# Tiles of exponentials that hold one tile of keys of two heads, and a nan made by multiplication

## The chip, the cores and the metric

The kernel runs on one core of a Trainium2 chip. The metric is the device time of one execution in microseconds; less is better. The engines are called as in the profile: PE (TensorE, matmuls), DVE (VectorE), ACT (ScalarE), POOL (GpSimd), SP (SyncE, which only issues DMAs).

## What is computed

Four batches of 512 tokens of width 256 go through four blocks of cross attention to 1024 context tokens and a feed-forward each. Cut to what matters here (names shortened):

```
x = x + tanh(g_xattn[0]) * attention0(layernorm(x), ctx)   # 16 heads of 16, 512 queries, 1024 keys
x = x + tanh(g_ffn[0])   * ffn0(layernorm(x))              # binarized weights, gelu
x = x + tanh(g_xattn[1]) * attention1(layernorm(x), ctx, mask)
x = x + tanh(g_ffn[1])   * ffn1(layernorm(x))              # x and weights to float8_e4m3fn, then a product
x = x + tanh(g_xattn[2]) * attention2(layernorm(x), ctx)   # one head
x = x + tanh(g_ffn[2])   * ffn2(layernorm(x))
x = x + tanh(g_xattn[3]) * attention3(layernorm(x), ctx)   # as attention0
x = x + tanh(g_ffn[3])   * ffn3(layernorm(x))              # six layers of local attention and a gated ffn

# attention0, 1, 3, for each batch and head:
scores = einsum('bhqd,bhkd->bhqk', q, k) / sqrt(16)        # layer 1: where(mask, scores, -inf)
ctx = einsum('bhqk,bhkd->bhqd', softmax(scores), v)

# ffn1, its quantization (beyond 464 the cast gives nan):
x_q = (x.astype(float32) / s_in).astype(float8_e4m3fn)
k_q = (kernel.astype(float32) / s_k).astype(float8_e4m3fn)
```

## The kernel before

The program has two parts. first_part computes everything up to the last block's cross attention, last_part the six layers of ffn3. Only first_part matters here.

**Units and groups.** The heads of layers 0, 1 and 3 are worked off in 12 units, one for each layer and batch, in that order; a unit has 4 groups of 4 heads. first_order writes the order of all work by hand: every step gets a turn (put), a unit has 64 turns, a group 16, and each engine's program walks through the same list and takes from it what is its own. Each turn of a group has one step M and one step E, where E runs LAG = 20 turns behind M.

- **M** (scores with queries on the partitions): two matmuls at L428 write 128 queries x 1024 keys of one head to a pair of PSUM banks; DVE takes the row maximum (L651, in layer 1 L648 with the mask added).
- **sh** (L438, L669, L671, two DMAs): the 16 x 128 maxima of a group are transposed, negated and written by DMA as two more rows of the stacked queries. E of that group needs them.
- **E** (scores with keys on the partitions, shifted by the maxima): two matmuls at L449, in layer 1 with the mask added by one more each (L452), fill a pair of PSUM banks, and ACT writes their exponentials, 128 x 1024, to one of six tiles of probs (L831). Before the change such a tile is **two tiles of 128 keys of one head**, 512 queries each.
- **PV** (L465): the product with the values, 32 columns of the array for each head, so that four heads lie side by side. A burst is eight matmuls (2 tiles of keys x 4 heads), each of which PE does in two passes, so it shows as x16. It needs four E tiles and comes after the sixth. A group has 4 bursts, all 12 units 192. The result lies in one bank (acc) until **T** (L838, ACT) copies it; then DVE shuffles and inverts the sums in four pieces (L678, **R** L684).

Three pairs of PSUM banks go round between M, E and two similar steps (plan for "two"), two single banks between PV and all the rest (plan for "one"). M and E alternate, so an E takes the pair of the M of two turns before, when DVE has its maximum, and an M the pair of the E of the turn before, when ACT has its exponentials.

**Fillers.** Between them stand the projections of the next unit (L410, then ACT L817, L821, L825), values (L418, DVE L623), the output projection (L474), layer norms (L382, L389, L398), and beside units 2 to 5 ffn0 (L489, L496), beside units 6 to 9 ffn1, attention2 and ffn2 (L504 to L561).

**quantize** (L566 on) turns 128 x 512 values into float8_e4m3fn on DVE, step by step, each after the one before: where a value is beyond 464 the result must be nan, and that is made by L581 (1 or 0), L583 (the reciprocal: 1 or infinity), L586 (the difference with itself: 0 or nan), L588 (added to the result). It runs nine times: once on ffn1's weights (step qw), and for each batch on two chunks of 512 (step q1), whose product is L504. A row maximum of M stands between the two of a batch in DVE's queue, and others behind them.

## Time and profile before

| | us |
|---|---|
| median of 3 runs | 5603.79 |
| lowest and highest | 5603.43, 5604.02 |
| profiled execution | 5599.21 |
| its span, first to last instruction | 5597.9 |
| PE busy in the span | 4956.6 (89%) |
| DVE busy | 3445.9 (62%) |
| ACT busy | 3134.1 (56%) |
| POOL busy | 2262.1 (40%) |

The span is that of the profiled execution alone, and the other times have no profile. The start of an instruction is in microseconds from the span's start. Idle time of an engine is counted from the end of its last instruction to the start of the next, and a matmul's end lies some way behind the start of the next one in a stream, so a stall of PE is longer than the idle time beside it. The granted clock is a share of 2.4 GHz: 0.50 is 1.2 GHz.

### The profile page before, as it was taken

What the parts mean: (1) busy time and instruction counts of PE and PEld (TensorE: products, weight loads), DVE (VectorE), ACT (ScalarE), POOL (GpSimd) and SP (SyncE); (2) the same over time, 40 slices, a digit from 0 to 9 for tenths busy, and PEclk for the clock granted to TensorE, in tenths of its full rate; (3) what the DMA queues carried; (4) which work ended last, traced back from release to release, by engine and by line L of the source; (5) the groups of instructions that cost most, each with busy time, mean ns of one, the idle gap of its engine ahead of it and who ended that gap; (6) DMA issues with size and microseconds to landing.
All of it is one profiled execution on the core that took longest, in us unless ns stands there. A gap on an engine that the chain in (4) does not pass through costs nothing.

```text
span 5597.9 us, 92896 instructions
## 1 busy us (share of the span) xinstructions
PE 4956.6 (89%) x35848; PEld 3090.5 (55%) x35848; DVE 3445.9 (62%) x6534; ACT 3134.1 (56%) x6626; POOL 2262.1 (40%) x2202
## 2 busy tenths in 40 slices
PE   5888889979797878886999999999999999999997
PEld 2233323334343433323877777777777777777775
DVE  4664556574756565674766666666666666666664
ACT  2554454434343434444767677666767776676762
POOL 1111011001010101103867676667767666676762
PEclk6999999989898988997999999999999999999998
DMA  4232223221221111321100000000000000000000
GB/s 100 45 58 46 41 51 63 39 60 41 55 45 40 35 40 38 56 33 36 34 13 18 21 20 20 18 19 25 19 21 20 20 18 19 24 20 17 20 13 31
DMA packets 125064, 189.00 MB, mean 34 GB/s; under 512 B 18800, under 2 KB 67568, under 8 KB 124400
## 3 DMA queue, kind: packets, MB, share of 16 engines
q1 hardware_dynamic: 124624, 183.06, 14.7%
q8 instruction: 285, 4.67, 0.4%
q14 instruction: 155, 1.27, 0.1%
HBM read 150.09 MB, written 32.51 MB: 33 GB/s over the span
## 4 chain that ended last, share of the span: by engine, by line
PE 65%; DVE 18%; ACT 9%; issue 5%; POOL 2%; DMA 1%; SPq 0%; DVEq 0%; ACTq 0%; POOLq 0%
PE psum L1210 15%; PE psum L1258 8%; PE psum L465 6%; PE psum L1259 4%; PE psum L428 4%; PE psum L449 3%; DVE maxes L651 3%; ACT probs L831 2%; PE psum L1267 2%; PE psum L1300 2%; PE psum L1291 2%; PE psum L410 2%; PE psum L1282 2%; PE psum L474 2%; DVE psum L1415 1%
## 5 line engine op out<-in xcount | busy, mean ns | idle before, releaser
L831 ACT ACTIVATE probs<-psum 128x1024 f32<-128x1024 f32 x768 | 767.3, 1020 | 674.2 <-PE psum L449 388.4
L651 DVE TENSOR_REDUCE maxes<-psum 128x1 f32<-128x1024 f32 x512 | 615.0, 1212 | 336.1 <-PE psum L428 332.2
L1401 DVE TENSOR_TENSOR lwork<-psum,rotary 128x512 f32<-128x512 f32 x384 | 265.2, 691 | 779.9 <-ACT lwork L1503 743.4
L1528 ACT ACTIVATE lprobs<-psum,small_stats,stats 128x128 f32<-128x128 f32 x1536 | 579.8, 460 | 196.9 <-DVE small_stats L1419 196.0
L1588 POOL TENSOR_TENSOR stats<-stats,minus_half 128x8 f32<-128x8 f32 x384 | 640.4, 1668 | 32.0
L1584 POOL TENSOR_TENSOR lwork<-lwork 128x512 f32<-128x512 f32 x384 | 493.1, 1284 | 328.6 <-DVE lwork L1403 328.6
L428 PE MATMUL psum<-stack 96*128 96x512 bf16 x1536 | 485.7, 399 | 152.8 <-ACT probs L831 121.5
L449 PE MATMUL psum<-stack 98*128 98x512 bf16 x1536 | 520.6, 395 | 107.8 <-DVE maxes L651 58.2
L930 POOL TENSOR_TENSOR attn<-attn,sums 128x512 f32<-128x512 f32 x48 | 60.8, 1266 | 1316.6 <-DVE sums L684 1316.6
L1503 ACT ACTIVATE lwork<-psum 128x512 f32<-128x512 f32 x384 | 231.2, 602 | 382.7 <-PE psum L1259 382.2
L648 DVE CUSTOM_DVE_ANT_0 psum<-psum,mask_by_query 128x1024 f32<-128x1024 f32 x256 | 314.0, 1229 | 195.8 <-PE psum L428 194.8
L1258 PE MATMUL psum<-wqkv_hi,xs_hi 128*128 128x512 f32 x768 | 339.8, 442 | 87.0 <-DVE att_lo L1433 43.5
L465 PE MATMUL psum<-probs,values 128*32 128x512 f32 x3072 | 397.4, 638 | 2.5 <-ACT probs L831 2.5
L428 PEld LDWEIGHTS psum<-stack 96*128 96x128 bf16 x1536 | 131.1, 100 | 433.5 <-ACT probs L831 227.2
L449 PEld LDWEIGHTS psum<-stack 98*128 98x128 bf16 x1536 | 141.1, 101 | 411.0 <-DVE maxes L651 126.9
L1258 PE MATMUL psum<-wqkv_hi,xs_lo 128*128 128x512 f32 x768 | 307.7, 401 | 0.0
L1258 PE MATMUL psum<-wqkv_lo,xs_hi 128*128 128x512 f32 x768 | 305.4, 398 | 0.0
L1300 PE MATMUL psum<-mixed_vals,turned 128*64 128x65 f32 x3072 | 261.0, 227 | 33.7 <-DVE lwork L1403 33.0
L1415 DVE TENSOR_REDUCE psum<-psum 128x4 f32<-128x512 f32 x384 | 265.3, 691 | 1.3 <-PE psum L1282 1.3
L1300 PEld LDWEIGHTS psum<-mixed_vals,turned 128*64 128x64 f32 x3072 | 207.8, 137 | 102.4 <-issue 53.4
L915 POOL TENSOR_TENSOR ln_stats<-ln_stats,minus_half 128x4 f32<-128x4 f32 x32 | 32.2, 1007 | 572.7 <-DVE ln_stats L609 572.7
L1409 DVE TENSOR_REDUCE stats<-lwork 128x8 f32<-128x512 f32 x384 | 263.3, 686 | 0.3 <-issue 0.3
(228 smaller groups left out, 12530.1 us busy)
## 6 DMA issues: line engine op xcount, KB each, us to landing
stack<-k_parts SPq DMA_DIRECT2D x288, 128.0 KB
staged<-in_quads SPq DMA_DIRECT2D x144, 256.0 KB, 2.4
k_parts<-parts SPq DMA_DIRECT2D x48, 384.0 KB, 2.8
stack<-q_parts SPq DMA_DIRECT2D x288, 64.0 KB
staged<-in_w SPq DMA_DIRECT2D x54, 256.0 KB, 2.7
ctx<-in_ctxT SPq DMA_DIRECT2D x24, 512.0 KB, 4.8
q_parts<-parts SPq DMA_DIRECT2D x24, 384.0 KB, 2.8
arena<-in_ctxT SPq DMA_DIRECT2D x8, 512.0 KB, 4.3
```

The costliest lines, as they stand in the source:

```text
L428: ins = tensor.matmul(ps[:, i, :], q[0:STACK, h, qt * P:(qt + 1) * P], k[0:STACK, h, i * S:(i + 1) * S], start=True, stop=True)
L449: ins = tensor.matmul(ps[:, i, :], ky[0:STACK + 2, h, kt * P:(kt + 1) * P], q[0:STACK + 2, h, :], start=True, stop=L != 1)
L465: ins = tensor.matmul(bank(acc)[32 * h:32 * h + 32, :], values[:, kt, 4 * g + h, :], pr, start=kt == 0, stop=kt == KT - 1)
L651: ins = vector.tensor_reduce(to, pair(("M", u)), AX.XY, ALU.max)
L831: scalar.activation(probs[:, i % 6, :, :], pair(("E", u)), ACT.Exp).then_inc(S_["E_act"], 1)
L1210: ins = tensor.matmul(ps, l, r, start=first and n == 0, stop=last and n == 2)
L1258: tensor.matmul(qk, x_[:, c, b % 2, tok(tt)], w_[:, c * COLS:c * COLS + 512], start=first, stop=last)
L1300: ins = tensor.matmul(bank(("pv", u, 0))[64 * w:64 * w + 64, h * (LHD + 1):(h + 1) * (LHD + 1)], pt[:, h, 64 * w:64 * w + 64], (va if w el ...
L1415: step(vector.tensor_reduce(top, scores(u), AX.X, ALU.max))
L1528: ins = scalar.activation(pr[:, h, :], scores(u)[:, h % 2, h // 2, :], ACT.Exp, bias=st[:, 4 + h:5 + h], scale=y[:, h:h + 1])
L1584: gpsimd.tensor_tensor(t1, t1, t2, ALU.add)
L1588: pool_step(gpsimd.tensor_tensor(st[:, 8:16], st[:, 0:8], minus_half[:, :], ALU.pow))
```

## The change

There are two edits, independent of each other.

**The tiles.** An E tile is now one tile of 128 keys of two heads (kt, and p for heads 2p and 2p + 1) in place of two tiles of keys of one head. So two E tiles, not four, complete a tile of keys for all four heads, and PV runs for each of the eight tiles of keys, four matmuls at a time, from two tiles of probs. Its turn is two behind the second E tile, as before: turn 2 kt + 3 of the group's E in place of 4 k + 5. ACT's wait for a free tile of probs, the values' and masks' waits and the loads' waits follow. T is written one turn earlier. The accumulator's bank is taken at the group's turn 3 in place of 5.

**The nan.** L581 gets a second operation, minus 1, so it gives 0 or -1; L583, the reciprocal, becomes a tensor_scalar that multiplies twice by 3e38, which gives 0 or minus infinity.

```diff
@@ -141,17 +141,17 @@
         put(16 * n - 12 if n > 2 else -1, ("st", u))
     for n, (L, b) in enumerate(UNITS):
         for i in range(64):
-            g, h, qt = i // 16, i % 16 // 4, i % 4
-            put(64 * n + i, ("M", (L, b, g, h, qt)))
-            put(64 * n + i + LAG, ("E", (L, b, g, h, qt)))
+            g, j = i // 16, i % 16
+            put(64 * n + i, ("M", (L, b, g, j // QT, j % QT)))
+            put(64 * n + i + LAG, ("E", (L, b, g, j // 2, j % 2)))
         for g in range(G4):
             t = 64 * n + 16 * g
             if L == 1:
                 put(t + 16, ("sha", (L, b, g)))
             put(t + 17, ("sh", (L, b, g)))
-            for k in range(KT // 2):
-                put(t + LAG + 4 * k + 5, ("PV", (L, b, g, k)))
-            put(t + LAG + 19, ("T", (L, b, g)))
+            for kt in range(KT):
+                put(t + LAG + 2 * kt + 3, ("PV", (L, b, g, kt)))
+            put(t + LAG + 18, ("T", (L, b, g)))
             for i in range(QT):
                 put(t + LAG + 20 + i, ("R", (L, b, g, i)))
         for k in range(KT // 2):
@@ -437,33 +437,31 @@
                     left(one, ("sh", u), PE)
                     tensor.transpose(bank(("sh", u))[0:16, 0:P], maxes[:, n % 4, 0:16], ident[:, :]).then_inc(S_["sh_pe"], 1)
                 elif stage == "E":
-                    L, b, g, k2, h = u
+                    L, b, g, kt, p = u
                     n = group_of[L, b, g]
                     PE.wait_ge(shift_in[n % 4], 32 * (n // 4 + 1))
                     if L == 1:
-                        PE.wait_ge(S_["mc_dve"], at_("mc", (b, 4 + k2)))
+                        PE.wait_ge(S_["mc_dve"], at_("mc", (b, 4 + kt // 2)))
                     left(two, ("E", u), PE)
                     ps, q, ky = pair(("E", u)), qst[n % 3], kst[n % 3]
                     for i in range(2):
-                        kt = 2 * k2 + i
+                        h = 2 * p + i
                         ins = tensor.matmul(ps[:, i, :], ky[0:STACK + 2, h, kt * P:(kt + 1) * P], q[0:STACK + 2, h, :],
                                             start=True, stop=L != 1)
                         if L == 1:
                             ins = tensor.matmul(ps[:, i, :], ident_b[:, :], masks_k[:, kt * S:(kt + 1) * S], start=False, stop=True)
                     ins.then_inc(S_["E_pe"], 1)
                 elif stage == "PV":
-                    L, b, g, k2 = u
-                    PE.wait_ge(S_["va_dve"], at_("va", (L, b, k2)))
-                    PE.wait_ge(S_["E_act"], at_("E", (L, b, g, k2, 3)))
+                    L, b, g, kt = u
+                    PE.wait_ge(S_["va_dve"], at_("va", (L, b, kt // 2)))
+                    PE.wait_ge(S_["E_act"], at_("E", (L, b, g, kt, 1)))
                     acc = ("acc", (L, b, g))
-                    if k2 == 0:
+                    if kt == 0:
                         left(one, acc, PE)
-                    for i in range(2):
-                        for h in range(4):
-                            kt = 2 * k2 + i
-                            pr = probs[:, tile_of((L, b, g, k2, h)) % 6, i, :]
-                            ins = tensor.matmul(bank(acc)[32 * h:32 * h + 32, :], values[:, kt, 4 * g + h, :], pr,
-                                                start=kt == 0, stop=kt == KT - 1)
+                    for h in range(4):
+                        pr = probs[:, tile_of((L, b, g, kt, h // 2)) % 6, h % 2, :]
+                        ins = tensor.matmul(bank(acc)[32 * h:32 * h + 32, :], values[:, kt, 4 * g + h, :], pr,
+                                            start=kt == 0, stop=kt == KT - 1)
                     ins.then_inc(S_["PV_pe"], 1)
                 elif stage == "wo":
                     L, b, m = u
@@ -578,9 +576,9 @@
             step.join()
             step(vector.scalar_tensor_tensor(out=big, in0=val, scalar=16.0, in1=big, op0=ALU.is_ge, op1=ALU.mult))
             step.join()
-            step(vector.tensor_scalar(val, val, 464.0, None, ALU.is_le))
+            step(vector.tensor_scalar(val, val, 464.0, 1.0, ALU.is_le, ALU.subtract))
             step.join()
-            vector.reciprocal(aux, val)
+            vector.tensor_scalar(aux, val, 3e38, 3e38, ALU.mult, ALU.mult)
             step(vector.tensor_tensor(big, big, lo8, ALU.add))
             step.join()
             step(vector.tensor_tensor(aux, aux, aux, ALU.subtract))
@@ -616,7 +614,7 @@
                     L, b, k2 = u
                     n = unit_of[L, b]
                     if n:
-                        V.wait_ge(S_["PV_pe"], at_("PV", UNITS[n - 1] + (3, k2)))
+                        V.wait_ge(S_["PV_pe"], at_("PV", UNITS[n - 1] + (3, 2 * k2 + 1)))
                     V.wait_ge(S_["va_pe"], at_("va", u))
                     for k in range(2):
                         heads = lambda x: x.rearrange("p (h d) -> p h d", h=H)
@@ -630,7 +628,7 @@
                     if b and i < 4:
                         V.wait_ge(S_["M_dve"], at_("M", (1, b - 1, 3, 3, i)))
                     elif b:
-                        V.wait_ge(S_["E_pe"], at_("E", (1, b - 1, 3, i - 4, 3)))
+                        V.wait_ge(S_["E_pe"], at_("E", (1, b - 1, 3, 2 * (i - 4) + 1, 1)))
                     dst = masks_q if i < 4 else masks_k
                     vector.tensor_scalar(dst[:, i % 4 * S2:(i % 4 + 1) * S2], mask_u8[:, j % 2, :], -1.0, -MASKED,
                                          ALU.add, ALU.mult).then_inc(S_["mc_dve"], 1)
@@ -827,12 +825,12 @@
                     i = tile_of(u)
                     A.wait_ge(S_["E_pe"], at_("E", u))
                     if i > 5:
-                        A.wait_ge(S_["PV_pe"], (i - 6) // 4 + 1)
+                        A.wait_ge(S_["PV_pe"], (i - 6) // 2 + 1)
                     scalar.activation(probs[:, i % 6, :, :], pair(("E", u)), ACT.Exp).then_inc(S_["E_act"], 1)
                 elif stage == "T":
                     L, b, g = u
                     n = group_of[u]
-                    A.wait_ge(S_["PV_pe"], at_("PV", (L, b, g, 3)))
+                    A.wait_ge(S_["PV_pe"], at_("PV", (L, b, g, KT - 1)))
                     if n > 3:
                         A.wait_ge(S_["wo_pe"], at_("wo", UNITS[n // 4 - 1] + (1,)))
                     scalar.activation(outs[:, g, :], bank(("acc", (L, b, g))), ACT.Copy).then_inc(S_["T_act"], 1)
@@ -975,7 +973,7 @@
                         i = at_("pj", (L, b, j)) - 1
                         SP.wait_ge(parts_out[i % 3], 16 * (i // 3 + 1))
                     if n > 2:
-                        SP.wait_ge(S_["E_pe"], at_("E", GROUPS[n - 3] + (3, 3)))
+                        SP.wait_ge(S_["E_pe"], at_("E", GROUPS[n - 3] + (KT - 1, 1)))
                     k, q = kst[n % 3], qst[n % 3]
                     rows = slice(g * 4 * HD, (g + 1) * 4 * HD)
                     for i, (pq, pk) in enumerate(PAIRS):
```

How the order on the engines changes, at three places.

PE in the first unit of layer 0, among the projections of the next one (L410), before; L449 is E, L428 is M:

```order
L410 MATMUL psum<-ctx,w_att 128x512 x2
L449 MATMUL psum<-stack 128x512 x2
L428 MATMUL psum<-stack 128x512 x2
L449 MATMUL psum<-stack 128x512 x2
L428 MATMUL psum<-stack 128x512 x2
L410 MATMUL psum<-ctx,w_att 128x512 x2
L449 MATMUL psum<-stack 128x512 x2
L428 MATMUL psum<-stack 128x512 x2
L449 MATMUL psum<-stack 128x512 x2
L428 MATMUL psum<-stack 128x512 x2
L465 MATMUL psum<-probs,values 32x512 x8
L410 MATMUL psum<-ctx,w_att 128x512 x2
```

and now (the bursts are L463):

```order
L410 MATMUL psum<-ctx,w_att 128x512 x2
L449 MATMUL psum<-stack 128x512 x2
L428 MATMUL psum<-stack 128x512 x2
L449 MATMUL psum<-stack 128x512 x2
L428 MATMUL psum<-stack 128x512 x2
L463 MATMUL psum<-probs,values 32x512 x4
L410 MATMUL psum<-ctx,w_att 128x512 x2
L449 MATMUL psum<-stack 128x512 x2
L428 MATMUL psum<-stack 128x512 x2
L449 MATMUL psum<-stack 128x512 x2
L428 MATMUL psum<-stack 128x512 x2
L463 MATMUL psum<-probs,values 32x512 x4
L410 MATMUL psum<-ctx,w_att 128x512 x2
```

The burst that stood ahead of every second projection is two, one ahead of each.

PE in the same unit, where no filler stands, before:

```order
L465 MATMUL psum<-probs,values 32x512 x8
L449 MATMUL psum<-stack 128x512 x2
L428 MATMUL psum<-stack 128x512 x2
L449 MATMUL psum<-stack 128x512 x2
L428 MATMUL psum<-stack 128x512 x2
L449 MATMUL psum<-stack 128x512 x2
L428 MATMUL psum<-stack 128x512 x2
L449 MATMUL psum<-stack 128x512 x2
L428 MATMUL psum<-stack 128x512 x2
L465 MATMUL psum<-probs,values 32x512 x8
```

and now:

```order
L463 MATMUL psum<-probs,values 32x512 x4
L449 MATMUL psum<-stack 128x512 x2
L428 MATMUL psum<-stack 128x512 x2
L449 MATMUL psum<-stack 128x512 x2
L428 MATMUL psum<-stack 128x512 x2
L463 MATMUL psum<-probs,values 32x512 x4
L449 MATMUL psum<-stack 128x512 x2
L428 MATMUL psum<-stack 128x512 x2
L449 MATMUL psum<-stack 128x512 x2
```

Between two bursts stand two E and two M in place of four of each, and a burst has half the matmuls.

DVE in the quantization of the weights, before:

```order
L579 SCALAR_TENSOR_TENSOR arena<-arena 128x512
L581 TENSOR_SCALAR arena<-arena 128x512
L583 RECIPROCAL arena<-arena 128x512
L584 TENSOR_TENSOR arena<-arena 128x512
L586 TENSOR_TENSOR arena<-arena 128x512
L588 TENSOR_TENSOR w_ffb<-arena 128x512
```

and now, where the lines are two less:

```order
L577 SCALAR_TENSOR_TENSOR arena<-arena 128x512
L579 TENSOR_SCALAR arena<-arena 128x512
L581 TENSOR_SCALAR arena<-arena 128x512
L582 TENSOR_TENSOR arena<-arena 128x512
L584 TENSOR_TENSOR arena<-arena 128x512
L586 TENSOR_TENSOR w_ffb<-arena 128x512
```

In place of L583's reciprocal stands L581's tensor_scalar; nothing else moved.

## Rows read from the trace of the kernel before

**Rows 1.** Stretch, its us; busy us of PE, PEld, DVE, ACT, POOL; granted clock, DMA share, GB/s

```profile
130.00:2565.00 2435.00, 2046.47 (x9384) 826.34 (x9383) 1493.81 (x2054) 1077.32 (x1254) 240.32 (x208) 0.94 0.24 46
```

**Rows 2.** What PE waited for, 130 to 2565 us: us in total, times, longest

```profile
PE psum L428 <- ACT probs L831: 121.5, 150, 2.3
PE psum L449 <- DVE maxes L651: 58.2, 65, 10.1
PE psum L449 <- DVE maxes L648: 26.5, 10, 9.7
PE psum L504 <- DVE arena L588: 22.6, 3, 8.1
...
PE psum L449 <- DMA stack<-shifts: 12.5, 12, 2.9
...
PE psum L438 <- DVE xn L605: 9.7, 1, 9.7
...
PE psum L504 <- issue: 7.3, 1, 7.3
```

**Rows 3.** Timeline of DVE in one quantization: start us, us; then all nine reciprocals

```profile
1461.30 0.42 DVE L572 TENSOR_SCALAR arena<-arena 128x512 f32<-128x512 f32 x1
...
1464.73 3.35 DVE L583 RECIPROCAL arena<-arena 128x512 f32<-128x512 f32 x1
1468.00 0.63 DVE L584 TENSOR_TENSOR arena<-arena 128x512 f32<-128x512 f32 x1
L583 DVE RECIPROCAL arena<-arena x9: 3353/3353/3354, 1165.5 to 2004.3; 128x512 f32<-128x512 f32 x9
```

**Rows 4.** Timeline of PE round a pair of quantizations: [idle before it, releaser]

```profile
1471.34 0.61 PE L449 MATMUL psum<-stack 98*128 98x512 bf16 x1 [9.69 <-DVE maxes L648]
...
1481.30 1.04 PE L504 MATMUL psum<-arena,w_ffb 128*128 128x512 bf16 x2 [7.22 <-DVE arena L588]
...
1484.94 3.24 PE L465 MATMUL psum<-probs,values 128*32 128x512 f32 x16
```

**Rows 5.** Timeline of PE (start us, us) over four stretches from burst to burst, layer 0

```profile
734.66 1.92 PE L465 MATMUL psum<-probs,values 128*32 128x512 f32 x16
...
748.62 1.92 PE L465 MATMUL psum<-probs,values 128*32 128x512 f32 x16
750.48 0.61 PE L449 MATMUL psum<-stack 98*128 98x512 bf16 x2
750.92 0.60 PE L428 MATMUL psum<-stack 96*128 96x512 bf16 x2
...
752.20 0.60 PE L428 MATMUL psum<-stack 96*128 96x512 bf16 x2 [0.25 <-ACT probs L831]
...
754.56 0.60 PE L428 MATMUL psum<-stack 96*128 96x512 bf16 x2
755.09 1.92 PE L465 MATMUL psum<-probs,values 128*32 128x512 f32 x16
...
762.64 0.64 PE L465 MATMUL psum<-probs,values 128*32 128x512 f32 x4
```

**Rows 6.** Timeline of PE, second and fourth round of the burst at 748.62

```profile
749.07 0.61 PE L465 MATMUL psum<-probs,values 128*32 128x512 f32 x4
...
749.93 0.61 PE L465 MATMUL psum<-probs,values 128*32 128x512 f32 x4
```

**Rows 7.** Timeline of PE among projections, behind a burst and without one

```profile
724.08 1.98 PE L410 MATMUL psum<-ctx,w_att 128*128 128x512 f32 x4
725.90 0.60 PE L449 MATMUL psum<-stack 98*128 98x512 bf16 x2
...
729.37 1.88 PE L410 MATMUL psum<-ctx,w_att 128*128 128x512 f32 x4
731.09 0.60 PE L449 MATMUL psum<-stack 98*128 98x512 bf16 x2
```

**Rows 8.** Columns as in rows 1, round the first quantization of the pair

```profile
1461.00:1471.00 10.00, 0.65 (x3) 0.10 (x1) 9.76 (x12) 1.51 (x2) 0.00 (x0) 0.64 0.33 37
```

## The prediction

> **What bounds the kernel now.** I read the busy time by stage, then who PE waits for, then the timelines of three places. The diff touches only the first part of the kernel, the attention units up to about 2565 us; behind it every instruction stays, and I leave those 3033 us of the span as they are. In the first part PE is busy for 2046 of 2435 us, and no other engine comes near: DVE 1494, ACT 1077 [rows 1]. So PE is the engine to follow, and what it does not spend on matmuls it spends waiting: 121.5 us for exponentials on ACT, in 150 waits of at most 2.3 us, and 58.2 and 26.5 us for row maxima on DVE, in which a few of about 10 us stand out [rows 2]. Those, with the waits of L504 and L438, are the quantization.
>
> **The reciprocal, step by step.** quantize runs nine times, once on weights and eight times on tokens, and the nine reciprocals last 3353 ns each. DVE starts L583 at 1464.73 and L584 at 1468.00: 3.27 us, 0.08 less than the duration. The replacement is a tensor_scalar with two immediate operations on the same 128x512 f32 in SBUF; L572 is exactly that form and lasts 0.42 us [rows 3]. With the same overlap 0.34 remains: a gain of 2.93 us each, 2.85 if the whole 0.42 counts. The second operation that L581 gets I put at nothing, since L572 carries two in its 0.42. Is this on the path? Round one batch's pair of chains PE is idle for 9.69 us, until a row maximum queued behind the chain on DVE is there, and then for 7.22, until L588, the chain's end, lets L504 go [rows 4]. The sums show the same for the others: L504 waits 22.6 us in three waits and 7.3 in a fourth, L438 9.7 in one, and the longest waits for L648 and L651 are 9.7 and 10.1 [rows 2]. As 2.93 is less than each, nothing else gets late first: PE still waits 6.8 and 4.3 us, for the same chain. So 9 x 2.93 = 26.3 us go; 25 at least.
>
> **What halving the bursts costs PE.** The work is equal: as many matmuls, exponentials and maxima, only the two halves of a tile are now two heads. But each burst of eight matmuls (16 passes in the profile) becomes two of four, each between matmuls of another array shape. In a row of score pairs one pair takes 0.44 us, start to start (750.48 to 750.92). From the last pair to a burst it is 0.53 (754.56 to 755.09): going in costs 0.09. The burst at 748.62 holds PE until 750.48, 1.86 us [rows 5]. Its second round of four passes starts at 749.07, its fourth at 749.93: 0.45 for the first round, 0.43 for the next two, and 0.55 from the last round's start to the next pair [rows 6]. So a burst of eight is 0.09 + 1.86 = 1.95 and one of four 0.09 + 0.45 + 0.55 = 1.09; two are 2.18. **0.23 us more, for each of 192 (12 units of 4 groups of 4), is 44 us.** Before an fp32 matmul over the full array there is more: L410 behind a burst keeps the next pair away for 1.82 us (724.08 to 725.90), without a burst for 1.72 (729.37 to 731.09) [rows 7]. In the order of the program about 76 bursts had such a filler behind them, and about 124 have one now: 48 times 0.10 is 5 us. Together 49 us, if nothing absorbs them.
>
> The Trainium skill, "TensorEngine Tiling (Array Packing)", Key Properties, says that changing the tiling mode drains TensorE, which speaks against this change. The trace agrees that a change costs, but a part of a tail each time. If each of the 384 new changes cost the whole tail of a pair (it lasts 0.60 and steps by 0.44, so 0.16), the term would be 61 us instead of 44.
>
> **What absorbs them.** Three pairs of PSUM banks go round between M (scores for the maxima, L428) and E (scores for the exponentials, L449). M of a turn needs the exponential of the turn before; E needs the maximum of two turns before. Without a filler four turns take 6.47 us (748.62 to 755.09), of which 4 x 0.88 + 1.95 = 5.47 is PE's own work. The other 1.0 are stalls, and the first is plain: E at 750.48 is followed by the M that needs its exponential at 752.20, 1.72 us later, where PE had 3 x 0.44 = 1.32 to do [rows 5]. All of them fall between bursts, while during a burst ACT and DVE run dry. Now each half is E M E M burst, with one such stall: 1.72 + 0.44 + 1.09 = 3.25 us, and four turns 6.50 instead of 6.47. So there nearly all of the 0.23 is absorbed. No new wait comes with it: a burst needs the exponential of two turns back, and the M ahead of it has already waited for a later one. The tiles come free before they are asked for, in both versions.
>
> Over a whole group more is absorbed. E of the next group waits for the shifts' DMA (12 waits, 12.5 us [rows 2]), and a half burst now lies in that time. The four slow reciprocals of the sums load DVE where a whole burst lets it run idle, and E then waits for its maxima. Four stretches, 734.66 to 762.64, take 28.0 us [rows 5]. Walking the same turns with halves, the DMA and the reciprocals put in, I get about 27.2: 0.8 less, though 4 x 0.23 of switching is in it. So a stretch without fillers absorbs 0.43. About 48 of the 192 are such, 21 us. Some 30 others have fillers in even turns only (feed-forward, values), where the half burst lands beside a stall; by the same walk 0.3 each, 9 us. The projections absorb nothing: PE stalls behind ACT's chain that begins with L410's end, whatever stood before L410. Nor do most stretches of layer 1, where the mask doubles E and PE is the bound, nor the dense middle. The accumulator opens two turns earlier and so meets the copy of the old one sooner; 3 us. Shorter stalls should also leave fewer short stretches at half clock; 6 us back (estimate, from a burst that takes 3.24 us there instead of 1.92 [rows 4, 5]). 49 - 21 - 9 + 3 - 6 = **16 us lost**, between -10 and +49. As the walk leans to less in the groups with sh, I take 14.
>
> **Sum.** -26.3 + 14 = -12 us. The profiled execution took 5599.2 us (span 5597.9 and 1.3 around it), 4.6 under the median of 5603.8; so 5587 there, and **5592** for the median.
>
> **Rivals.** (a) The switches are hardly absorbed: fillers lie beside so many bursts that only plain stretches give, and half of what I think. 49 - 11 = 38, less 26 is +12; with nothing absorbed +23. So 5616 to 5627, slower. It decides once the bursts' net loss passes 37.5 us (26.3, and 11.2 for 0.2%). For it: the projections' stall lies behind the filler. Against: the stalls of rows 5 lie where the new bursts go. (b) The loss is about what the reciprocal gives, 20 to 30 us: 5598 to 5608, no change. (c) Even feeding wins beyond my walk, in the dense middle too: attention -10, in all -36, 5568. For it: 121 and 58 us of waits are to be had [rows 2]. (d) The clock. Between the two idle times of a pair, and for some 6 us behind the second, PE works at half clock: the burst at 1484.94 takes 3.24 us [rows 4]. If idle times of 6.8 and 4.3 us let it stay at 2.4 GHz, half of some 2.7 + 6 us is won, four times: 18 more, 5574. Against: over 1461 to 1471 the mean granted clock is 0.64, which is 1.2 GHz from the third microsecond on [rows 8], long before an idle time of 6.8 us would end. The Trainium skill, "TensorE: Matmul & The Clock Gate", What's actually happening, points the same way: low is the default, and activity lifts it. That the change does not do what it says is no rival, since the order shows both edits.
>
> **Chances.** A measurement of this kernel can tell 0.2%, 11 us, from no change. My case, -20 to -3: 0.50, a little over half of it beyond 11 us. (a) 0.12, (b) 0.15, (c) 0.15, (d) 0.08. Faster: 0.27 + 0.15 + 0.08 = 0.50. Same: 0.23 + 0.15 = 0.38. Slower: 0.12. The range for 8 in 10 leaves out most of (a) and the far end of (c): 5573 to 5612; my own case alone is 5584 to 5601.
>
> **What would show it.** The new L581 (L583 before) near 0.42 us nine times, and idle times of 6.8 and 4.3: else the first term is wrong. A burst of four that begins 0.53 after the last pair and lets the next one start 1.00 later: else the 0.23. Four turns without a filler at 6.5 us, one stall of 0.25 (as the profile counts idle time) in each half: else the walk. The wait for the shifts' DMA nearly gone, and fewer stretches at half clock. If the part behind 2565 is not 3033 us long again, something else is at work.

## The result, and the profile after

| | before | after |
|---|---|---|
| median, us | 5603.91 | 5533.12 (4 runs, 5529.55 to 5538.01) |
| ratio to before | | 0.9873, 95% interval 0.986 to 0.9885 |
| profiled execution | 5599.21 | 5534.83 |
| its span | 5597.9 | 5533.5 |

The change takes 70.8 us away. I had forecast 12, and the range ended at 5573: wrong by 59 us, in the good direction.

The stretch of the first part, columns as in rows 1:

```profile
130.00:2500.00 2370.00, 2059.33 (x9320) 795.24 (x9383) 1468.13 (x2053) 1078.17 (x1254) 239.95 (x208) 0.95 0.25 47
```

It is 65 us shorter (130 to 2565 before), and PE is busy for 13 us more in it than in rows 1. So PE lost waits, not work. What it waited for in that stretch, which answers to rows 2:

```profile
PE psum L428 <- ACT probs L829: 107.6, 146, 2.2
PE psum L449 <- DVE maxes L649: 33.9, 25, 6.7
PE psum L449 <- DVE maxes L646: 19.0, 7, 6.3
PE psum L502 <- DVE arena L586: 14.4, 3, 5.6
...
PE psum L438 <- DVE xn L603: 8.1, 3, 7.3
```

The waits of E (L449) for row maxima fell from 75 to 32 and from 84.7 us to 52.9; those of M (L428) for ACT by 14 us. The new nan step, and PE round the same pair of quantizations as in rows 3 and 4:

```profile
L581 DVE TENSOR_SCALAR arena<-arena x9: 426/427/427, 1165.1 to 1976.1; 128x512 f32<-128x512 f32 x9
```

```profile
1458.00 0.61 PE L449 MATMUL psum<-stack 98*128 98x512 bf16 x1 [6.33 <-DVE maxes L646]
...
1465.09 1.04 PE L502 MATMUL psum<-arena,w_ffb 128*128 128x512 bf16 x2 [4.35 <-DVE arena L586]
...
1468.11 1.94 PE L463 MATMUL psum<-probs,values 128*32 128x512 f32 x8
```

0.43 us in place of 3.35, and idle times of 6.33 and 4.35 where I had written 6.8 and 4.3. The burst behind the second still takes 1.94 us, where one at full clock takes 1.06. Four stretches without a filler, answering to rows 5 and 6:

```profile
738.30 1.07 PE L463 MATMUL psum<-probs,values 128*32 128x512 f32 x8
739.29 0.60 PE L449 MATMUL psum<-stack 98*128 98x512 bf16 x2
739.74 0.60 PE L428 MATMUL psum<-stack 96*128 96x512 bf16 x2
740.17 0.60 PE L449 MATMUL psum<-stack 98*128 98x512 bf16 x2
741.02 0.60 PE L428 MATMUL psum<-stack 96*128 96x512 bf16 x2 [0.25 <-ACT probs L829]
741.55 1.07 PE L463 MATMUL psum<-probs,values 128*32 128x512 f32 x8
742.55 0.28 PE L438 MATMUL psum<-ident,maxes 128*16 128x128 f32 x1
...
748.65 1.06 PE L463 MATMUL psum<-probs,values 128*32 128x512 f32 x8
...
751.90 0.64 PE L463 MATMUL psum<-probs,values 128*32 128x512 f32 x4
```

The burst comes 0.53 us behind the last pair (741.02), holds PE for 1.00, and two turns take 3.25 us (738.30 to 741.55, 748.65 to 751.90) with one stall of 0.25. All as walked through. And L410 behind a burst keeps the next pair away for 1.82 us, as in rows 7:

```profile
715.29 1.98 PE L410 MATMUL psum<-ctx,w_att 128*128 128x512 f32 x4
717.11 0.60 PE L449 MATMUL psum<-stack 98*128 98x512 bf16 x2
```

**Where the gain is seen.** It can be read in the last unit (batch 3 of layer 3): PE from L382 to the burst behind L398. Before:

```profile
2400.71 1.88 PE L382 MATMUL psum<-x_resid,ones_mean 128*128 128x512 f32 x4
...
2406.06 1.03 PE L428 MATMUL psum<-stack 96*128 96x512 bf16 x2 [2.17 <-ACT probs L831]
2406.88 1.06 PE L449 MATMUL psum<-stack 98*128 98x512 bf16 x2
2407.87 2.57 PE L465 MATMUL psum<-probs,values 128*32 128x512 f32 x16
...
2417.46 0.60 PE L449 MATMUL psum<-stack 98*128 98x512 bf16 x2 [1.31 <-DVE maxes L651]
2417.99 1.92 PE L465 MATMUL psum<-probs,values 128*32 128x512 f32 x16
```

and DVE beside it:

```profile
2407.13 1.23 DVE L651 TENSOR_REDUCE maxes<-psum 128x1 f32<-128x1024 f32 x1 [2.08 <-PE psum L428]
2411.02 2.36 DVE L651 TENSOR_REDUCE maxes<-psum 128x1 f32<-128x1024 f32 x2 [2.67 <-PE psum L428]
...
2415.57 0.01 DVE L678 LOAD_MASK_SELECT sums<-attn  x1 [1.84 <-ACT attn L838]
...
2416.20 1.20 DVE L651 TENSOR_REDUCE maxes<-psum 128x1 f32<-128x1024 f32 x1
```

After:

```profile
2353.14 1.88 PE L382 MATMUL psum<-x_resid,ones_mean 128*128 128x512 f32 x4
...
2358.49 0.60 PE L428 MATMUL psum<-stack 96*128 96x512 bf16 x2 [1.07 <-ACT probs L829]
...
2366.30 0.60 PE L398 MATMUL psum<-ident,ln_stats 128*128 128x128 f32 x4
2366.92 0.61 PE L449 MATMUL psum<-stack 98*128 98x512 bf16 x2
2367.45 1.07 PE L463 MATMUL psum<-probs,values 128*32 128x512 f32 x8
```

From L382 to the burst behind L398 the same 7 E, 6 M and fillers take 17.3 us with 8 matmuls of values before, and 14.3 with 12 of them after. Before, DVE runs dry for 2.67 us while the long burst is on PE. E's wait of 1.31 us further on is no lack of DVE's time, though: DVE stands idle for 1.84 us ahead of L678, until ACT has copied the accumulator (T), and the maximum that E needs (2416.20) is queued behind that shuffle. Over the first part, seven waits for maxima of 9.9 us in all stand behind a shuffle that waits for T, and six of 2.5 us with the tiles only (worked out from the two traces). The stall of 2.17 us is 1.07, and what follows is no longer at half clock: before, M, E and the burst behind the stall took 1.03, 1.06 and 2.57 us, against 0.60, 0.60 and 1.92 elsewhere. The clock in these places (columns as in rows 1), before and after:

```profile
2406.00:2410.00 4.00, 3.94 (x20) 0.95 (x20) 1.23 (x1) 1.94 (x3) 0.00 (x0) 0.59 1.13 121
```

```profile
2359.00:2363.00 4.00, 4.00 (x29) 2.11 (x28) 2.45 (x2) 2.84 (x4) 0.00 (x0) 1.00 1.12 130
```

**An account for every kernel.** The time from the first matmul of an M (62.9 us in the kernel before) to the first matmul of the last part (2613.4 us) is cut in three, all worked out from the trace: PE's idle time; what is lost at half clock (half of PE's busy time in the stretches at 1.2 GHz); the rest, PE's work at full clock. A matmul followed by a stall counts its 0.16 us of tail as work, so fewer stalls also make the work look smaller.

| us, first M to last part | idle | lost at half clock | work | sum |
|---|---|---|---|---|
| before | 443.9 | 137.5 | 1969.0 | 2550.5 |
| tiles only | 386.5 | 126.8 | 2001.1 | 2514.4 |
| nan only | 418.1 | 134.6 | 1969.0 | 2521.6 |
| both (the change) | 366.5 | 120.9 | 1996.7 | 2484.4 |
| both, run again | 361.8 | 123.9 | 2001.3 | 2487.0 |

The trace of the change lacks 65 matmul records of the first part, 64 of them of L452, which the trace of its repeat has. Leaving the same ones out of the repeat moves some 5 us from work to idle time, about the difference between the last two rows. The traces with 44 eights, with fours in half of the units and with one step less in the nan (further down) lack them too, so their idle time and work compare with the change, and with the others within some 5 us.

### The profile page after: what moved, and what is told of

It reads as the page before. It is cut to its first block, busy times and chain, and to the rows that moved or that the text cites. A ratio compares the mean times of both kernels' runs of the same rounds, so it can differ in the third digit from the quotient of the medians.

```text
span 5533.5 us, 92962 instructions
## 1 busy us (share of the span) xinstructions
PE 4968.7 (90%) x35783; PEld 3059.1 (55%) x35848; DVE 3420.0 (62%) x6534; ACT 3134.8 (57%) x6626; POOL 2263.3 (41%) x2202
## 4 chain that ended last, share of the span: by engine, by line
PE 65%; DVE 17%; ACT 9%; issue 6%; POOL 2%; DMA 1%; SPq 0%; DVEq 0%; ACTq 0%; POOLq 0%
PE psum L1208 15%; PE psum L1256 8%; PE psum L463 5%; PE psum L428 4%; PE psum L1257 4%; PE psum L449 3%; DVE maxes L649 3%; ACT probs L829 3%; PE psum L1265 2%; PE psum L1298 2%; PE psum L410 2%; PE psum L1289 2%; PE psum L1280 2%; PE psum L472 2%; DVE psum L1413 1%
## 5 line engine op out<-in xcount | busy, mean ns | idle before, releaser
L428 PE MATMUL psum<-stack 96*128 96x512 bf16 x1536 | 488.1, 401 | 139.4 <-ACT probs L829 107.6
L449 PE MATMUL psum<-stack 98*128 98x512 bf16 x1536 | 521.1, 395 | 69.6 <-DVE maxes L649 33.9
L463 PE MATMUL psum<-probs,values 128*32 128x512 f32 x3072 | 430.8, 634 | 1.3 <-ACT probs L829 0.6
L428 PEld LDWEIGHTS psum<-stack 96*128 96x128 bf16 x1536 | 130.4, 101 | 452.0 <-ACT probs L829 206.9
L449 PEld LDWEIGHTS psum<-stack 98*128 98x128 bf16 x1536 | 140.8, 101 | 410.0 <-issue 161.9
L918 POOL TENSOR_TENSOR work<-work,parts 128x512 f32<-128x512 f32 x72 | 83.9, 1166 | 453.8 <-ACT parts L819 453.8
L1514 ACT ACTIVATE queries<-psum 128x256 f32<-128x256 f32 x384 | 143.9, 375 | 213.5 <-PE psum L1265 203.9
```

The source lines that it names most:

```text
L428: ins = tensor.matmul(ps[:, i, :], q[0:STACK, h, qt * P:(qt + 1) * P], k[0:STACK, h, i * S:(i + 1) * S], start=True, stop=True)
L449: ins = tensor.matmul(ps[:, i, :], ky[0:STACK + 2, h, kt * P:(kt + 1) * P], q[0:STACK + 2, h, :], start=True, stop=L != 1)
L463: ins = tensor.matmul(bank(acc)[32 * h:32 * h + 32, :], values[:, kt, 4 * g + h, :], pr, start=kt == 0, stop=kt == KT - 1)
```

## The experiments

Medians are compared with the kernel before on the same chip (5605.2 us in the first four, 5605.1, 5602.3 and 5601.0 in the later groups of four), with the 95% interval of the ratio.

**The two halves of the change.** Tiles only:

```diff
-            step(vector.tensor_scalar(val, val, 464.0, 1.0, ALU.is_le, ALU.subtract))
+            step(vector.tensor_scalar(val, val, 464.0, None, ALU.is_le))
             step.join()
-            vector.tensor_scalar(aux, val, 3e38, 3e38, ALU.mult, ALU.mult)
+            vector.reciprocal(aux, val)
```

> The new tiles and the bursts of four, with the reciprocal kept in quantize. Theory S (the prediction's price of the reciprocal was right, its price of the tiles was wrong): the reciprocal gives 26 us, so this kernel stands about 45 us below the kernel before, near 5559. Theory N (the prediction's price of the tiles, a loss of 14 us, was right and all the rest is the reciprocal, through the clock): 14 us slower than before, near 5618. Theory C (in between: the shorter idle times in quantize also give back clock, some 10 us): 35 us faster, near 5569.

5565.98 us, 0.993 (0.9917 to 0.9944): 39 us less. Nan only, the same lines the other way round on the kernel before:

> The kernel before with the reciprocal of quantize made a multiplication, tiles and bursts as before. Theory S: 26 us faster, near 5578. Theory N: 85 us faster, near 5519. Theory C: 26 us and some 10 of clock, 36 us faster, near 5568; the stretches at half clock round the pairs of chains are then 14 to 17 us long in place of 20 to 24.

5573.64 us, 0.9941 (0.9929 to 0.9954): 31.5 us less. In the account the idle time falls by 25.8 and the half-clock loss by 2.9. The medians' two gains add up to 70.7 us, the whole gain. The nan was priced right (26.3 forecast; the interval of its 31.5 reaches from 26 to 40); the tiles were not even of the right sign.

**New tiles, old bursts.** Bursts of eight at their old turns, tiles-only kernel:

```diff
-                put(t + LAG + 2 * kt + 3, ("PV", (L, b, g, kt)))
-            put(t + LAG + 18, ("T", (L, b, g)))
+                put(t + LAG + 4 * (kt // 2) + 5, ("PV", (L, b, g, kt)))
+            put(t + LAG + 19, ("T", (L, b, g)))
```

> The new tiles, but two products with values back to back at the old turns, so that the bursts have eight matmuls as before, and the copy of the accumulator at its old turn; the reciprocal kept. If the gain of the tiles comes from the bursts of four standing between the pairs of score matmuls, it is gone here: within 5 us of the kernel before. If it comes from anything else in the new tiles (what is read, when tiles come free), it stays: as e1.

5599.96 us, 0.9991 (0.9982 to 0.9999). Of the 39 us, 5 are left (0.6 to 10), hardly clear of the noise, and the waits are those of rows 2 again:

```profile
PE psum L428 <- ACT probs L829: 121.5, 150, 2.3
PE psum L449 <- DVE maxes L649: 58.4, 65, 10.1
PE psum L449 <- DVE maxes L646: 26.5, 10, 9.7
```

So some 34 of the 39 us come from splitting the bursts and from what went with it (the halves' turns, and T one turn earlier, which this run put back too), and little or nothing from the tiles' layout. No run moves T alone.

**Two reciprocals**, the kernel before with the reciprocal twice:

```diff
             step(vector.tensor_scalar(val, val, 464.0, None, ALU.is_le))
+            step.join()
+            step(vector.reciprocal(aux, val))
             step.join()
             vector.reciprocal(aux, val)
```

> The kernel before with the reciprocal in quantize done twice, 3.35 us more in each of nine chains. If a microsecond of the chain is a microsecond of the kernel, with no help from the clock (theory S): 30 us slower, near 5634. If the longer idle time costs clock too (theories C and N): 40 us or more.

5626.91 us, 1.0042 (1.0028 to 1.0055): 22 us more (16 to 31) for 30 us of DVE: theory S's 30 lies at the edge, the clock's 40 outside. PE's idle time grows by 30.3 us (to 474.2), so DVE's chain is on its path one for one; 6.3 us less are lost at half clock (131.2), although PE idles more.

**Eights beside projections.** The changed kernel with

```diff
-                put(t + LAG + 2 * kt + 3, ("PV", (L, b, g, kt)))
+                eight = n < 11 and (g == 0 and kt > 3 or g == 1 and kt < 4)
+                put(t + LAG + (4 * (kt // 2) + 5 if eight else 2 * kt + 3), ("PV", (L, b, g, kt)))
```

> The changed kernel (5533), with bursts of eight put back in 44 places: in the four stretches of each unit in which projections of the next unit (L410) stand between score pairs. Bursts of four everywhere else, and the cheap nan. Summed over stretches of four turns, the traces of before and of the tiles-only kernel show 18.3 us MORE for the tiles where projections stand (33 stretches), and 47 us less in all others. Theory P (projections absorb nothing, as predicted; the gain lies in the other stretches): each of the 44 gives back 0.23 to 0.33 us, 10 to 15 us, 18 at most: 5515 to 5523. Rival (the even feeding pays there too, or the growth beside projections is only where the trace puts the boundary): no gain, 5530 to 5545.

5533.23 us (0.9873, 0.9858 to 0.9888), the same as with fours. The account is 370.9 idle, 124.5 lost, 1983.8 work: 12.9 us less work for 44 bursts, 0.29 each, and I had priced 0.23, or 0.33 with a filler behind. So the price of switching is right, and beside projections little absorbs it (4.4 us of idle time come back). Half clock (3.6) and what lies outside the account (3.7 us longer in this trace) hide the rest, so as a gain it is not shown.

**Fours in half of the units**, the changed kernel with `eight = n > 5` (fours in units 0 to 5) and `eight = n < 6` (fours in 6 to 11) in the same line:

> The changed kernel with bursts of eight in units 6 to 11, of four in units 0 to 5 only; the cheap nan everywhere, so it lies between the nan-only kernel (5573.6) and the changed one (5533.1). By unit, the trace of the tiles-only kernel puts only 4 to 9 us of the gain in units 0 to 5. Theory (the gain lies where feed-forward, attention2, values and norms stand beside the scores, and in the last units): 5565 to 5570. Rival (the gain is spread evenly over all bursts, and the units' own times only carry it along): half of 40, 5553.

> The other half: bursts of four in units 6 to 11 only, eight in units 0 to 5, the cheap nan. Theory: nearly all of the tiles' gain is here, 5537 to 5542. Rival (spread evenly): 5553. If the two halves do not add up to the whole (40 us from 5573.6 to 5533.1), units feed on each other.

5550.48 us (0.9906, 0.9891 to 0.9921) and 5552.92 (0.9908, 0.9893 to 0.9923). Each half brings 21 to 23 of the 40 us: my reading by unit was wrong, the rival was right. The traces tell more. Against nan-only, the first kernel has 22.0 us less idle time and 9.9 less lost at half clock, for 12.0 more work (with the missing records some 27 less and 17 more); but of its 20.1 us only 3.5 lie in units 0 to 5. The other 16.6 lie behind unit 5, where the order hardly changed (unit 5's last bursts stand beside unit 6), 6.0 of them at half clock. What one unit leaves behind moves the waits and the clock of later ones, so where in a trace a gain lies does not say which edit made it. How it carries over that far I can't say.

**One step less in the nan**, on the changed kernel:

```diff
-            step(vector.tensor_tensor(aux, aux, aux, ALU.subtract))
             step.join()
-            return vector.tensor_tensor(dst, big, aux, ALU.add)
+            return vector.scalar_tensor_tensor(out=dst, in0=aux, scalar=0.0, in1=big, op0=ALU.mult, op1=ALU.add)
```

> The changed kernel with one step less in the quantization: the difference of aux with itself (L582 to L584, 128x512 f32, 0.63 us by the trace) goes, and the last step multiplies aux by 0 and adds it to the result in one scalar_tensor_tensor: 0 times minus infinity is nan. Theory (each 1 us out of the nine chains on DVE is 1 us of the kernel, as the reciprocal was, 9 x 2.93 forecast): 9 x 0.6 = 5.4 less, 5527 to 5528. Rival (the last step gets slower in its new form, or the idle time has found another owner): 5531 to 5536.

5519.42 us (0.9853, 0.9836 to 0.9869): 13.7 less, more than either theory. In the trace the idle time falls by 5.8, about what nine steps of 0.68 should give, and the half-clock loss by 18.3 (to 102.6). But the profiled execution was the fastest of four, 5513.39 us, so the 18.3 is more than a typical execution gains. With the eights beside projections as well:

> The kernel with the step less in the quantization (5519.4), and with bursts of eight in the 44 places beside projections. The run that put those eights back alone left the median where it was (5533.2), though its trace shows 12.9 us less PE work at full clock and 4.4 us more idle time up to the last part, 8.5 us net; 3.6 us more lost at half clock and 3.7 us more in the last part took most of that back. Theory (the 8.5 are real, the rest is how the half-clock stretches fall, which another run draws anew): 5511, 5504 to 5518. Rival (what the eights save in switching always comes back as half clock, since PE then idles more): 5517 to 5523.

5516.36 us (0.9844, 0.983 to 0.9858), inside theory's range and 1 us short of the rival's, with 3 us between it and the kernel without eights: not told apart. Work and idle time are 11.2 us less, and the half-clock loss is back at 123.7.

**Half maxima.** Is DVE, starved in a burst and behind after it, what the small bursts mend? In the kernel before, and in tiles-only, the row maximum of layers 0 and 3 leaves out the second half of the keys:

```diff
-                        ins = vector.tensor_reduce(to, pair(("M", u)), AX.XY, ALU.max)
+                        ins = vector.tensor_reduce(to, pair(("M", u))[:, 0, :], AX.X, ALU.max)
```

> The kernel before (5605), where in layers 0 and 3 the row maximum is taken over the first 512 of the 1024 keys only (the second half is left out of it): 512 maxima on DVE from 1.22 us to about 0.69 (what a reduction of 128x512 from PSUM takes elsewhere in the trace). PE waits 59 us in 86 waits for these maxima, some 20 of it behind quantizations. Theory D (bursts of eight starve E of maxima: four score turns are 3.5 us of PE and 4.9 of DVE, and DVE catches up only in the burst; the smaller bursts remove these waits): 20 to 35 us less here, 5570 to 5585. Rival (the waits for maxima only stand in for others, ACT's next): 0 to 10 us less.

> The same half maxima with the new tiles and bursts of four (and the reciprocal of before), so tiles-only (5566) with short maxima. To be compared with the kernel before with half maxima, which runs beside it. Theory D: most of what the new tiles gain (39 us) is waits for maxima that are gone here anyway (27 to 30 us of them in the traces), so the new tiles gain only 5 to 20 us in this pair. Rival (the gain comes from ACT's stalls, from half-clock stretches or from elsewhere): 30 to 40 us, as with full maxima.

5519.78 us (0.9857, 0.9844 to 0.9871) and 5501.75 (0.9819, 0.9806 to 0.9833). With maxima of 0.69 us the new tiles gain 18 us, with maxima of 1.22 they gain 39. So about half of the gain hangs on how long the maxima take, as theory D has it; that it is the backlog behind a burst, and not DVE being less loaded everywhere, these runs do not show. What is left in this pair is idle time 401.1 to 363.0, half clock 105.3 to 94.1, work 32 more. The waits of the two, old bursts first:

```profile
PE psum L428 <- ACT probs L831: 126.1, 172, 2.3
PE psum L449 <- DVE maxes L648: 26.5, 11, 9.7
PE psum L449 <- DVE maxes L651: 25.4, 12, 9.2
```

```profile
PE psum L428 <- ACT probs L829: 112.2, 167, 2.2
PE psum L449 <- DVE maxes L646: 24.8, 7, 9.2
PE psum L502 <- DVE arena L586: 22.6, 3, 8.1
PE psum L449 <- DVE maxes L649: 22.0, 7, 9.1
```

12 waits for the shortened maxima (L651) are left against 65, and 18 of their 25.4 us are four waits behind quantizations; of the other half of the gain, 14 us are stalls behind ACT. The short maxima alone gave 82 us where I expected 20 to 35: idle time -42.8, half clock -32.2. I had counted the visible waits only.

**The burst between E and M.** The stall left in each pair of turns stands ahead of M. The changed kernel, with each PV moved ahead of its turn's M:

```diff
+    for parts in turn.values():
+        late = [p for p in parts if p[0] == "PV"]
+        if late and any(p[0] == "M" for p in parts):
+            parts[:] = [p for p in parts if p[0] != "PV"]
+            i = [p[0] for p in parts].index("M")
+            parts[i:i] = late
```

> The changed kernel (5533.1) with each burst of four one place earlier in its turn: between E and M, not behind M. PE still waits 108 us in 156 waits for M until ACT has the exponential of the turn before. In a plain pair of turns that M comes 3 score pairs (1.32 us) behind the E it waits for, which takes 1.72; with the burst in between it is 1.32 + 1.0, and no M waits: two turns are 4 x 0.44 + 1.09 = 2.85 us in place of 3.25. Theory (the stall is in the order of E, M and burst): the waits of M for ACT fall from 108 to some 50 to 70, and the kernel by 25 to 50 us: 5483 to 5508. Rival 1 (with PE faster, DVE's maxima at 1.22 us each and the sums' reciprocals at 0.94 set the pace: 2 x 1.22 + 0.47 = 2.9 us for two turns): waits of E for maxima grow by 20 to 40 us and little is left, 5520 to 5535. Rival 2 (the burst, earlier, waits for its own exponential): slower than 5535.

5506.06 us (0.9826, 0.9813 to 0.984), 27 less than the changed kernel. Its waits (L434 is M, L455 is E):

```profile
PE psum L455 <- DVE maxes L655: 63.2, 88, 6.7
PE psum L434 <- ACT probs L835: 44.1, 61, 1.5
PE psum L455 <- DVE maxes L652: 19.5, 8, 6.3
```

The stalls behind ACT fell from 107.6 to 44.1 us; 30 us of waits for maxima took part of their place, as rival 1 said, and the rest is what theory said. Half clock: 101.4.

> New tiles, cheap nan, and all bursts of eight again, but between E and M. To be set beside the kernels with eights behind M (nan-only, 5573.6), fours behind M (5533.1) and fours ahead of M (5506.1). Theory (small bursts are what counts: a burst of eight covers the stall of one M in four, one of four of one in two): half of the 27 us that the place gave, and none of the 40 of the halving: 5555 to 5565. Rival (the place alone does it, and halving only pays the switches): 5510 or less.

The same move with `eight = True`: 5590.51 us (0.9982, 0.9973 to 0.9992). That is 17 us more than nan-only (23 by the ratios), which neither theory had, and 84 more than fours in that place. M's stalls behind ACT are 81.8 us, but E waits 95.5 for maxima and 158.6 us are lost at half clock. So splitting is worth 84 us there, 40 behind M. The place alone does nothing good.

**Together**, the burst ahead of M and the step less:

> Both things that helped, together: bursts of four between E and M (5506.1 alone), and the step less in the quantization (5519.4 alone, 13.7 under the changed kernel, of which 5.4 to 8 are the step itself by the trace and the rest half clock). Theory (independent: one is DVE's chain, the other PE's stalls behind ACT): 5492 to 5501. Rival (in the turns beside the quantization the maxima set the pace, so the shorter chain is the same gain again): 5503 to 5508.

> The same with bursts of eight in the 44 places beside projections, also between E and M. When the bursts stood behind M, those eights took 12.9 us of PE work away and gave 4.4 back as idle time. Theory S (only the switching counts there): 8 us less than its pair without eights. Theory O (ahead of M a burst of four covers a stall behind ACT in every second turn, 49 us of stalls beside projections having become 17; with eights every second of those M stalls again): 5 to 20 us more.

5501.79 us (0.9821, 0.9806 to 0.9836) and, with eights beside projections, 5520.79 (0.986, 0.9843 to 0.9876). The first is the best here that leaves nothing out: 99 us under the kernel before, 31 under the change. It lies between the two expectations; the step brings 4 more, which is within the noise of the two medians. The second is 19 us worse (theory O): work is 9.1 less, but idle time 15.4 and half clock 19.1 more.

**The changed kernel once more:**

> The changed kernel itself once more, not altered. By the traces, 120.9 us of its first part are lost at half clock, against 137.5 before. If that loss is set by the order of the work, it is 118 to 124 again and the time 5530 to 5537; if it falls anew in each execution, it may be anywhere from 110 to 135, and 10 us of any pair of kernels can be chance.

5533.12 us (0.9877, 0.9862 to 0.9892), 123.9 us lost at half clock against 120.9. New tiles with old bursts had 136.7 against 137.5 before. That looks as if one order repeated its loss within about 3 us, but the executions without a trace say otherwise. Over the eight of the changed kernel the mean granted clock was 0.962 to 0.966, and the time 5525.8 to 5538.8 us; both profiled ones stood at 0.962. A step of 0.004 in 5530 us is some 22 us of such loss, if idle time at half clock is counted too (estimate). So the rival is right in part: the loss also falls anew in each execution. Nan-only's five stood at 0.959 to 0.960, below all eight, so that the change loses less than nan-only does belong to the order; the 14 us are the difference of two traces.

## Why the prediction was wrong

- **The reciprocal: right.** 2.93 us of each of nine were on the path: 25.8 us less idle time, forecast 26.3. The clock gave only 2.9 us there: rival (d)'s 18 did not come, since the clock had fallen long before the idle times ended: PE's last matmul ended at 1451.67, the granted clock is 0.97 over 1452 to 1454 and 0.50 from 1454 on, and the idle time of 6.33 us ended at 1458.00.
- **The price of switching: right where it could be isolated.** 0.53 and 1.00 us round a burst, 0.29 us each for 44 bursts. (Counted in the traces, a filler stands right behind 53 bursts before and 101 after, not 76 and 124; the difference of 48, which the sum uses, is right.) The whole work grew by 32 us, not 49; fewer tails counted as work explain some of that (90 idle times fewer, at 0.16 each, 14 us). The Trainium skill, "TensorEngine Tiling (Array Packing)", Key Properties, has a change of tiling mode drain TensorE. By the run with 44 eights one burst more, with its change in and out, costs 0.29 us, whatever part of it is the drain; that was no reason against the change.
- **"What absorbs them": this step failed.** It took 33 us off the 49 to reach +16, and the measured sum is -39. Over stretches of four turns, before against tiles-only: 53 without a filler lose 14.9 us (0.28 each; I had a net 0.2), right. 33 with projections grow by 18.4: "the projections absorb nothing" is right too. **105 with other fillers lose 32.3 us, where I had some 30 of them absorb 9 in all, and layer 1 and the dense middle nothing.** (The remaining 7 us lie behind the last of these stretches. The stretches are cut at the first M of each four turns; cut at another turn, those without a filler lose 14 to 19, those with projections grow by 5 to 12, and the others lose 18 to 27. The signs stay, the sizes depend on the cut.) I had walked only through plain turns, and turned "PE is the bound there" into "nothing to absorb". The traces show what the splitting takes away instead: PE idles for 57 us less in tiles-only, of which 20 are waits of E for maxima (84.7 to 64.3), 15 stalls of M behind ACT (121.5 to 106.9) and 8 waits for the shifts' DMA (12.5 to 4.7). The stretches with other fillers hold the irregular work of DVE (norms, copies, shuffles, reciprocals). A burst of eight leaves DVE idle for 2 us or more (2.67 in the example), and behind it DVE is asked for four maxima of 1.22 us in four turns of 0.88 us of PE; bursts of four ask for two at a time. The half maxima put about half of the gain on the length of the maxima; that the backlog is the way it works there is argued, not shown.
- **The clock was a term, not a remainder.** I put 6 us; it was 10.7 in tiles-only and 16.6 in the whole change. The stall of 2.17 us at 2406.06 had half clock behind it, the one of 1.07 in its place had not, so a stall saved can pay more than its length. The Trainium skill, "TensorE: Matmul & The Clock Gate", What's actually happening, takes the low clock for the default, which activity lifts; the account of the change agrees: with 77 us less idle time (82 by the repeat, whose records are whole), the loss fell from 137.5 to 120.9 us. But idle time alone does not set it: with the reciprocal twice PE idled 30.3 us more and lost 6.3 less.
- **Rival (c)** had the mechanism, even feeding in the dense middle too, and 0.15. Its size, 10 us of gain, was a quarter of the real one, and I had nothing to size it by, though 84.7 us of waits for maxima stood in rows 2. (a) and (b) fell with the sign.
- **The rest of the list:** the part behind is as long as before (3033 us from 2500 on). The waits for the shifts' DMA fell to 4.5 us.

Open: why the gain of one half of the units shows up in the other half's time; how the 18 us that the tiles still gain with short maxima divide between ACT, DMA and the clock; and what T's earlier turn gives by itself.

## What to carry to other kernels

Where an engine that feeds PE is idle during a long block of PE's and behind after it, splitting the block can be worth more than the switches it costs (here 39 us net, switches paid). Sum the feeder's work between two blocks and compare it with PE's there, in the stretches with irregular work above all, and take all waits for that feeder as a first measure of what can be had, though not as its bound: shorter maxima gained 82 us where the waits for them were 58.2. Then put the split block ahead of the instruction that still stalls. Price a stall with the half-clock time that the trace shows behind it. And look at the granted clock of every execution, not of the profiled one alone, before a difference in half-clock loss is put down to an edit.

## What the runs showed of the hardware that I had not expected

- Half clock often amplifies, but not by a fixed rate. Shorter maxima took 42.8 us of idle time away and 32.2 of half-clock loss; nine steps less on DVE 5.8 and 18.3, in a trace of that kernel's fastest execution; the reciprocal twice added 30.3 us of idle time and took 6.3 of loss away. Over these kernels the loss ran from 94 to 159 us of some 2500 (with full maxima from 98). Two traces of one order agreed within 3 us, but over eight executions of it the mean granted clock ran from 0.962 to 0.966.
- The same matmuls in bursts of eight or of four, in two places of the turn, gave 5573.6, 5533.1, 5590.5 and 5506.1 us: the place made it worse with eights and better with fours.
